# Reordering the operand splits, layer statistics, a query product and the output bias in a two-layer gated cross-attention kernel

## The reference

```python
x = x + tanh(g_xattn[0]) * L0_xattn(layernorm(x), ctx, Wq, bq, Wkv, bkv, Wo, bo)
x = x + tanh(g_ffn[0])   * L0_ffn(layernorm(x), w_gate_up, w_down)        # silu(gate) * up, 1376 wide
x = x + tanh(g_xattn[1]) * L1_xattn(layernorm(x), ctx, Wq, Wk, Wv, Wo, q_norm_w, k_norm_w)
x = x + tanh(g_ffn[1])   * L1_ffn(layernorm(x), base_W, gate_W, lora_A, lora_B)   # top-2 of 28 experts, rank 8
```

## Time and profile before

| | |
|---|---|
| median of 3 runs | 1410.93 us (1410.56 to 1411.52) |
| the profiled execution's own time | 1412.08 us |
| its span in the profile | 1410.3 us |
| TensorE's mean granted clock | 0.995 |
| PE busy | 1372.8 us, 97% of the span |
| DVE / ACT / POOL busy | 1050.7 / 803.8 / 487.4 us |
| DMA | 63.82 MB, mean 45 GB/s |
| chain that ended last | PE 77%, DVE 12%, ACT 5%, POOL 3% |

### The profile page before, as it was taken

One profiled execution on the slowest core, in us unless ns is written; L12 is line 12 of the kernel. 1 busy time (PEld: TensorE's weight loads), 2 busy tenths in 40 slices (PEclk: granted clock), 3 DMA queues, 4 the chain that ended last, 5 costly groups with the idle time before them and its releaser, 6 DMA issues.

```text
span 1410.3 us, 23780 instructions
## 1 busy us (share of the span) xinstructions
PE 1372.8 (97%) x7976; PEld 1193.5 (85%) x7976; DVE 1050.7 (75%) x2739; ACT 803.8 (57%) x2227; POOL 487.4 (35%) x615
## 2 busy tenths in 40 slices
PE   5999999999999998999999999999999999999998
PEld 5899999988888887888888888888888888888777
DVE  7777787778824447788787787787788778778875
ACT  6787787775402215565565555556556556556641
POOL 5865565555825512212212222122222221212220
PEclk9999999999999999999999999999999999999999
DMA  5221122221312300100101001001001001000001
GB/s 202 76 76 49 70 74 74 74 76 45 121 46 60 116 1 16 61 1 33 44 0 74 1 1 74 0 0 74 0 0 74 0 0 74 15 30 14 1 9 53
DMA packets 14942, 63.82 MB, mean 45 GB/s; under 512 B 1760, under 2 KB 1760, under 8 KB 10656
## 3 DMA queue, kind: packets, MB, share of 16 engines
q1 hardware_dynamic: 14880, 63.07, 12.7%
HBM read 60.97 MB, written 2.10 MB: 45 GB/s over the span
## 4 chain that ended last, share of the span: by engine, by line
PE 77%; DVE 12%; ACT 5%; POOL 3%; issue 2%; DMA 0%; ACTq 0%; SPq 0%; DVEq 0%; POOLq 0%
PE psum L58 23%; PE psum L60 22%; PE psum L59 22%; PE psum L1427 3%; ACT p L1294 2%; PE psum L1438 2%; DVE mx L1095 1%; DVE w1q_lo L1053 1%; PE psum L1459 1%; DVE VW_lo L362 1%; POOL w0q_lo L240 1%; DVE qT_lo L1090 1%; DVE pT_lo L1060 1%; PE psum L1422 1%; PE psum L111 1%
## 5 line engine op out<-in xcount | busy, mean ns | idle before, releaser
L1294 ACT ACTIVATE p<-psum,nb,rq 128x320 f32<-128x320 f32 x256 | 155.3, 614 | 156.6 <-DVE nb L1099 156.6
L1021 POOL TENSOR_TENSOR p<-p,rinv 128x640 f32<-128x640 f32 x64 | 80.2, 1254 | 203.5 <-DVE rinv L1105 203.5
L58 PE MATMUL psum<-w1q_hi,xnT_lo 128*128 128x512 f32 x288 | 119.6, 415 | 0.0
L60 PE MATMUL psum<-w1q_hi,xnT_hi 128*128 128x512 f32 x288 | 113.3, 394 | 0.0
L59 PE MATMUL psum<-w1q_lo,xnT_hi 128*128 128x512 f32 x288 | 112.7, 391 | 0.0
L1271 ACT ACTIVATE pT_hi<-psum 128x512 fp32r<-128x512 f32 x128 | 69.7, 596 | 69.0 <-PE psum L1427 69.0
L1060 DVE TENSOR_TENSOR pT_lo<-psum,pT_hi 128x512 fp32r<-128x512 f32 x128 | 85.2, 686 | 30.9 <-ACT pT_hi L1271 30.2
L1095 DVE TENSOR_REDUCE mx<-psum 128x2 f32<-128x640 f32 x128 | 104.5, 816 | 3.9 <-PE psum L60 3.9
L60 PE MATMUL psum<-w1o_hi,oT_hi 128*128 128x512 f32 x256 | 100.5, 393 | 0.0
L59 PE MATMUL psum<-w1o_lo,oT_hi 128*128 128x512 f32 x256 | 100.5, 393 | 0.0
L58 PE MATMUL psum<-w1o_hi,oT_lo 128*128 128x512 f32 x256 | 100.1, 391 | 0.0
(11 more groups left out here) (237 smaller groups left out, 4642.0 us busy)
## 6 DMA issues: line engine op xcount, KB each, us to landing
raw_q<-in_w0q SPq DMA_DIRECT2D x8, 1024.0 KB, 4.7
raw_o<-in_w0o SPq DMA_DIRECT2D x8, 1024.0 KB, 4.8
raw_q<-in_w1q SPq DMA_DIRECT2D x8, 1024.0 KB, 7.5
raw_o<-in_w1o SPq DMA_DIRECT2D x8, 1024.0 KB, 4.8
raw_kv<-in_w_gu SPq DMA_DIRECT2D x10, 512.0 KB, 3.5
raw_gu<-in_w_gu SPq DMA_DIRECT2D x10, 512.0 KB, 3.5
raw_kv<-in_w0kv SPq DMA_DIRECT2D x8, 515.0 KB, 3.4
raw_kv<-in_w1kv SPq DMA_DIRECT2D x8, 512.0 KB, 5.5
```

What stands on the lines that cost most here:

```text
L58: pe.matmul(out, w[1], m[0], start=start, stop=False)
L60: return pe.matmul(out, w[0], m[0], start=False, stop=stop)
L1021: pool.tensor_tensor(p, p, k.rinv[:, stat(j)].unsqueeze(2).to_broadcast([PART, 2, KEYS]), ALU.mult).then_inc(p_scaled_pool, 1)
L1294: last = act.activation(k.p1[:, tile, 2 * hp + hh, :], s_pair(j)[:, hh, :], ACT.Exp, bias=k.nb[:, i:i + 1], scale=k.rq[:, i:i + 1], accum_ ...
```

## The change

Four edits, whose core is shown below (the loop variable that `q_proj` is given changes from n to g, and its callers with it):

- Attention 1, DVE: q piece 3 of the next group is no longer split at the end of unit b = 3, but in the next unit (b = 0, or the tail), after `cx_lo` and ahead of `t_lo` 3 (in the tail ahead of `t_lo` 2). PE waits for each q piece ahead of the matmuls that read it.
- The last norm's statistics go from units b = 2, 3 to the ends of units b = 1, 2.
- First units: unit 0 takes `q_lo` of tile 0 ahead of the squares of tile 1; unit 1's first query product runs on PE ahead of `turn` 2.
- Attention 0, POOL: all output-weight pieces of group 0 come after the eighth reciprocal deviation; the bias is added in the last group instead of group 0.

```diff
@@ attn0_phase, gpsimd, body
                 elif t >= 3:
                     ln.pool_rstd(pool, 1, t - 3)
-                if isinstance(g, int) and g == 0:
+                if not nxt:
+                    pool.wait_ge(x_done, NT * (NKV - 1))
                     pool.tensor_tensor(k.x[:, t, :], k.x[:, t, :], k.gbo[:, :], ALU.add).then_inc(bo_added, 1)
@@ attn0_phase, gpsimd, ahead of group 0
         for t in range(NT):
             ln.pool_rstd(pool, 0, t)
-            if t == 6:
-                pool.wait_ge(o_in, 16)
-                hi_piece("o", 0)
-                lo_piece("o", 0, 0)
-        for i in range(1, CONV["o"]):
+        pool.wait_ge(o_in, 16)
+        for i in range(CONV["o"]):
             hi_piece("o", i)
             lo_piece("o", 0, i)
-        pool.wait_ge(gbo_done, 1)
-        pool.wait_ge(ln.xn, NT)
         body(0, True)
...
+        pool.wait_ge(gbo_done, 1)
         body(NKV - 1, False)
@@ attn0_phase, vector, x_add
-            if isinstance(g, int) and g == 0:
+            if isinstance(g, int) and g == 0 and t == 0:
+                dve.wait_ge(gates, 1)
+            if isinstance(g, int) and g == NKV - 1:
                 dve.wait_ge(bo_added, t + 1)
@@ attn1_phase, vector, body
                 if b % 2 == 0:
                     cx_lo(g, b)
+                if prev and b == 0:
+                    w_lo("q", g, CONV["q"] - 1)
                 if prev:
                     t_lo(u, b, 3)
...
                     pv_lo(u, b, 0)
-                if not nxt and b >= 2:
-                    ln.dve_stats(dve, 3, 2 * b - 4)
-                    ln.dve_stats(dve, 3, 2 * b - 3)
...
+                if not prev:
+                    q_lo(n, b, 0, True)
                 q_squares(n, 1)
-                q_lo(n, b, 0, not prev)
+                if prev:
+                    q_lo(n, b, 0)
...
                     x_add(u, b, 1)
-                for c in conv[5:6]:
-                    w_lo(*c)
                 t_lo(n, b, 0)
                 row_max(n, 3)
                 t_lo(n, b, 1)
+                if not nxt and b in (1, 2):
+                    dve.wait_ge(x_added, 2 * u + 2)
+                    ln.dve_stats(dve, 3, 2 * b - 2)
+                    ln.dve_stats(dve, 3, 2 * b - 1)
@@ attn1_phase, vector, tail
             ln.dve_lo(dve, *ln_tiles(u)[1], ln_bank(BATCH - 1, 1))
+            w_lo("q", NKV, CONV["q"] - 1)
             t_lo(u, 0, 2)
@@ attn1_phase, tensor
+        def q_proj(g, b, tile, alone=False):
             t = 2 * b + tile
             for c in range(CH):
+                if b == 0 and tile == 0:
+                    pe.wait_ge(q_wlo, CONV["q"] * g + c + 1)
...
                 else:
+                    pe.wait_ge(kv_split, n + 1)
+                    q_proj(g, b, 0)
                     turn(u, b, 2)
...
-                if b == 0:
-                    pe.wait_ge(q_wlo, CONV["q"] * (g + 1))
                 if b % 2 == 0 and prev:
                     pe.wait_ge(cx_split, 2 * g + b // 2 + 1)
-                else:
+                elif not (first and b == 1):
                     pe.wait_ge(kv_split, n + 1)
-                q_proj(n, b, 0, not prev)
+                if not (first and b == 1):
+                    q_proj(g, b, 0, not prev)
@@ Ffn1, pe_base
-        if s == 0:
-            pe.wait_ge(self.free["q"], self.conv["q"] * (NKV + 1))
...
         for c in range(CH):
+            if s == 0:
+                pe.wait_ge(self.free["q"], self.conv["q"] * NKV + c + 1)
             mm3(pe, self.o_bank[s % 3], [w[:, c, tok] for w in k.xnT], [w[:, c, :] for w in k.w_base], c == 0, False)
```

More of the change, by code:

```diff
@@ L1447, in out @@
             last.then_inc(d_full, 1)
-        def q_proj(n, b, tile, alone=False):
+        def q_proj(g, b, tile, alone=False):
             t = 2 * b + tile
             for c in range(CH):
+                if b == 0 and tile == 0:
+                    pe.wait_ge(q_wlo, CONV["q"] * g + c + 1)
                 last = mm3(pe, y_bank(b, "q", tile, alone)[:, :], [w[:, c, t * PART:(t + 1) * PART] for w in k.xnT],
@@ L1545, in body @@
                     pe.wait_ge(pv_split, 2 * u + 1)
-                    q_proj(n, b, 1)
+                    q_proj(g, b, 1)
                     pe.wait_ge(kt_split, n + 1)
@@ L1549, in body @@
                     pe.wait_ge(cx_split, 1)
-                    q_proj(n, b, 1, True)
+                    q_proj(g, b, 1, True)
                 q_turn(n, b, 0, not prev)
```

## The result

The changed kernel takes 1403.2 us (median of 6 executions, 1401.86 to 1403.65), the kernel before 1411.22 us in the same set (1409.12 to 1411.7): a ratio of 0.9945, 95% interval 0.9932 to 0.9957. It is 8.0 us, 0.55%, faster; the prediction was 1400.1 us, range 1396.8 to 1404.5. The two profiled executions (1412.08 and 1401.86 us, spans 1410.3 and 1400.0) stand 10.2 us apart, not 8.0. Both numbers have to be explained.

What follows compares the result with a forecast made beforehand. PE, busy 97% of the span, was taken as the bound, leaving its idle and half-clock time to save. Six steps summed to 10.8 us, taken from 1410.93 (the profiled 1412.08 less 1.15): 1400.1 us, range 1396.8 to 1404.5.

Steps and rivals of the forecast that it cites:

- Step 1: Attention 1's seven group boundaries: moving q piece 3 removes PE's v_lo waits and is hidden in its new place, 5.7 us gained.
- Step 2: Last pair of transposes after unit 31: the norm transpose's wait goes as the piece moves into the tail, 0.95 us gained.
- Step 3: Attention 1's first two units: early q_lo costs 0.25 us, the early query product fills PE's hole; 2.0 us gained net.
- Step 4: Front of attention 0: first transpose 0.7 us earlier, set by POOL's queue; group 0 without bias additions, 0.6 us more.
- Step 5: Bias in group 7: POOL's idle time covers the additions except ahead of the last scaling, 0.45 us lost.
- Step 6: Units 30 and 31: earlier norm statistics remove PE's score waits, less delays at v_lo and t_lo 2; 1.3 us gained.
- the clock falls in the new gap: Rival, unit 1: PE's clock falls in the new 2 us gap, costing up to 2.98 us: 1403.1 us; chance 0.17.
- slow piece: Rival, boundaries: the piece takes 1.32 us in its new place, 0.5 us lost a boundary: 1403.6 us; chance 0.10.
- boundary wait: Rival, boundaries: the wait stays because ACT's evacuations hold v_lo; only 5.1 us gained: 1405.8 us; chance 0.04.
- gain beyond the sum: Rival: front keeps its clock, POOL's queue is shorter, unit 1 has no new gap; 3 us more, 1397; chance 0.07.
- wait for keys in b = 0: Sign of a wrong forecast; rival there: unit b = 0 becomes bound by DVE, slower than before, 1415.6 us; chance 0.02.

Runs made afterwards that it cites:

- E-piece: Kernel before with only the last q piece's move and the chunk waits of the q and base products: 1405.24 us, ratio 0.996.
- E-stats: Kernel before with only the four statistics of attention 1's last group moved: 1409.7 against 1411.0 us, ratio 0.9993.
- E-hoist: Kernel before with only unit 1's first query product moved ahead of turn 2: 1409.9 against 1411.0 us, ratio 0.9995.
- E-nohoist: Changed kernel with unit 1's first query product back behind its turns: 1404.21 us.
- E-attn0: Kernel before with only the changed POOL order in front of attention 0 and in groups 0 and 7: 1410.28 against 1411.0 us, ratio 0.9997.
- E-same: Changed kernel run once more, unaltered: 1403.55 us, ratio 0.9946.
- E-unit0: Changed kernel with unit 0's q_lo behind the squares again: 1403.08 us.
- E-bias: Changed kernel with group 7's bias additions moved: three ahead of the first scaling, the rest behind scalings 0, 1, 3, 4 and 5: 1404.47 us.
- E-tail: Changed kernel with the base weights' last piece split at the end of unit 31, ahead of its last scaling: 1400.86 us.

## Why the prediction was right, and where it was off

The range held and the sign was sure; the point was 3.1 us too low. Step by step:

- **Step 1, the boundaries (5.7).** Right: 5.98 us by E-piece alone. The reason was right as well: the piece costs 0.69 us in its new place and is hidden there.
- **Step 2, the last transposes (0.95).** The gain is there: 0.96 by E-piece, and 0.95 between E-stats (1343.50 - 1321.54 = 21.96 us) and the changed kernel (21.01). What failed is "the piece moves into the tail, where DVE has idle time ahead of pv_lo". The idle time was real, but ahead of another instruction. The piece should have been placed in DVE's order against the moment when PE takes the fourth chunk: 2.3 us after the base product starts, until when DVE has the scaling, six small operations and xnT_lo to do. And the scaling took 0.83 us more than before, beside POOL's subtraction, which the step did not count. Cost 1.44 us, net -0.5 instead of +0.95.
- **Step 3, the first two units (2.0).** The two profiles show 2.2 (48.32 to 46.14), the wait of 2.05 us at the keys is where it was said, and unit 0's 0.26 was costed at 0.25. But the 2.0 was not the worth of the edit, and that the profiles meet it is luck. It is 0.4 between executions that keep their clock and -0.5 to 1.0 between such that don't; by the medians about 1 (E-hoist 1.1, E-nohoist 0.7 to 1.0), not clear of the scatter. The rest is one execution of before that paid for a fall which E-attn0, with the same order there, didn't pay. I had taken the half clock behind 545 us for a property of the order, so I counted all it cost as the edit's gain.
- **Step 4 (0.7 and 0.6).** 0.64 at the first transpose and 1.02 at the end of group 0, so 0.4 for the second; the first is good to 0.6, the second doesn't depend on where the trace starts (21.79 us between the two steps before, 21.41 after). That PE's clock doesn't matter at the front, since POOL's queue sets the transpose, is shown by E-same: clock 1.00 from 30 to 36 us, and a transpose that waits 1.62 us for POOL and comes at 39.45.
- **Step 5 (-0.45).** 1.02 - 0.69 = 0.33 lost.
- **Step 6 (1.3).** About 1.4 by E-stats.
- **The steps together.** 5.98 - 0.49 + 2.18 + 0.64 + 0.38 - 0.33 + 1.36 = 9.7 us, where the profiles differ by 10.2; the half microsecond left is within what the loop scatters by.
- **From the profile to the median.** Against the profiled execution the sum said 1401.3, and the trace has 1401.86. That is 0.6 of the miss of 3.1; the other 2.5 are 1.15 that I took off and 1.34 between the profiled execution and the median. The median is 1403.2, because I took off 1.15 us for the execution of before and counted the end of its fall again in step 3, and took the changed kernel's course with no fall in unit 1 as its usual one. That is the rival "the clock falls in the new gap", which I gave 0.17 and priced at 1403.1. It was no either-or: the same wait of 2.05 us is followed by a fall in E-unit0, E-hoist and E-bias and not in the changed kernel's two profiles and E-tail's, and the medians (1403.2 and 1403.55) lie where the executions with one would. For executions without a profile the place of their fall is inferred, not seen: a fall in front of attention 0 alone gave 0.997 at 1401.86 us, so the mean clock doesn't tell it. The Trainium skill, "TensorE: Matmul & The Clock Gate", Part 1, says that the point of transition varies between runs of one kernel. The two executions of the changed kernel agree, and go further: in front of attention 0 the fall is there in one and not in the other.
- The other rivals fell: no slow piece (0.69 us), no boundary wait left, no gain beyond the sum, no wait for keys in b = 0.

What stays open: what decides in an execution whether the clock falls, why E-tail kept its clock in four of five executions with the wait of 2.06 us in place, and the 0.7 us that kernels with the same loop differ by over seven groups.

## What to carry to other kernels

A filler that closes one hole opens another if the same engine chain (here DVE's pT_lo, then keys) must still run behind it; look what that engine has queued, and reorder there: one pair of DVE instructions put ahead of two that wait was worth about as much as the moved product at a full clock (0.5 us and 0.4), and the spread went from 2.4 to 1.0 us with it. Don't price an edit by a pair of executions that differ in granted clock: find the same stretch at the same clock in some other kernel's trace. And a piece moved in a steady loop is moved at the loop's end too: place it there against the instruction that takes it, on its own.

## What the runs showed of the hardware

The granted clock fell in unit 1 in some profiled executions and not in others of the same instruction order, and for different lengths: before, PE was at 0.50 from 545.15 to 551.10, in E-piece, with the same order there, it was back at 1.00 by 549; behind the wait of 2.05 us of the changed order it fell in E-hoist, E-unit0 and E-bias, and not in the changed kernel's two profiles and E-tail's. In front of attention 0 it fell to 0.68 (30 to 33 us) in the changed kernel's first profiled execution and stayed at 1.00 in E-same, which is the same kernel. No stand of PE in unit 1 was longer than 2.06 us.

DVE's last scaling, a pair of 128x320, took 1.51 us in the changed kernel's tail (1.51 or 1.52 in E-same, E-piece and E-tail) and 0.68 in the kernel before; it started beside POOL's subtraction of 1.30 us there, while before POOL had finished its own (1346.53 + 1.26 us) ahead of the scaling's start at 1348.16. It has one input in SBUF, not two. By the Trainium skill, "SBUF — State Buffer", "SBUF: two separate sides", a DVE operation in its two-port mode and a POOL operation lock each other out for a whole instruction; the 0.83 us more are in line with that, and no run here shows it by itself.
